# A graph network on one core: slots are released by VectorE's additions, and TensorE posts once per part of its sums

## The reference, cut to what matters

```python
q = (h @ Wq.T + bq)[dst]; k = (h @ Wk.T + bk)[src]; v = (h @ Wv.T + bv)[src]
alpha = jnp.sum(q * k, axis=-1) / 4.0          # per head, 8 heads of 16
ex = jnp.exp(alpha - segment_max(alpha, dst)[dst])
out = segment_sum(ex / segment_sum(ex, dst)[dst] * v, dst)
```

## Time and profile before

| | us |
|---|---|
| timed runs, median of 3 | 5662.24 (5661.85 to 5665.38) |
| profiled execution, span from first to last instruction | 7864.5 |

### The profile page before, as it was taken

The page is one execution under the profiler, slowest core; times in us unless marked ns, Lnnn a source line. Parts: engine busy times, 40 slices in busy tenths (PEclk is TensorE's granted clock), DMA queues, the critical chain, the costliest instruction groups (busy, mean ns, idle before and its releaser), DMA issues.

```text
span 7864.5 us, 105863 instructions
## 1 busy us (share of the span) xinstructions
PE 4591.8 (58%) x22799; PEld 3687.8 (47%) x22800; DVE 4054.1 (52%) x11127; ACT 2762.9 (35%) x6393; POOL 3848.5 (49%) x4061
## 2 busy tenths in 40 slices
PE   4555555655555556555555565555555655666666
PEld 2444444534444445344444453444444544555555
DVE  4555555645555556455555564555555653333334
ACT  1333333423333334233333342333333432333333
POOL 3555555335555553345555543455555425555553
PEclk6666666676666666766666667666666677878788
DMA  4222222122222222222222222222222211111111
GB/s 127 78 78 74 78 78 77 52 66 76 78 77 79 76 79 57 65 69 77 77 79 77 79 61 68 68 78 78 78 76 80 60 31 44 44 45 45 45 44 27
DMA packets 267185, 536.12 MB, mean 68 GB/s; under 512 B 116251, under 2 KB 148687, under 8 KB 266507
## 3 DMA queue, kind: packets, MB, share of 16 engines
q0 software_dynamic: 180992, 490.24, 23.2%
q1 hardware_dynamic: 78899, 35.89, 1.8%
q10 hardware_dynamic: 6936, 6.69, 0.3%
HBM read 512.41 MB, written 18.03 MB: 67 GB/s over the span
## 4 chain that ended last, share of the span: by engine, by line
PE 27%; another core or an unknown queue 25%; issue 20%; DVE 17%; ACT 5%; DVEq 4%; ACTq 1%; DMA 0%; SPq 0%; POOL 0%; POOLq 0%
PE bank L765 9%; PE bank L784 8%; DVE acc L1191 6%; PE bank L769 2%; PE bank L756 2%; ACT oh L549 2%; DVEq L330 2%; PE bank L805 2%; PE bank L833 1%; DVE alpha L1214 1%; DVEq L1191 1%; DVE slots L1283 1%; DVE oh L1175 1%; PE bank L937 1%
## 5 line engine op out<-in xcount | busy, mean ns | idle before, releaser
L504 POOL DMA_INDIRECT slots<-kv_table,idx x3224 | 3065.0, 951 | 3149.1 <-PE bank L784 1272.7
L784 PE MATMUL bank<-slots,oh 128*128 128x136 f32 (+1 forms) x8060 | 1598.6, 352 | 584.7 <-DVE acc L1191 502.7
L765 PE MATMUL bank<-qs,ohT 128*128 x8080 | 1676.3, 354 | 230.3 <-ACT ohT L540 132.0
L784 PEld LDWEIGHTS bank<-slots,oh 128*128 128x128 f32 x8060 | 1415.4, 253 | 716.9 <-DVE acc L1191 614.8
L765 PEld LDWEIGHTS bank<-qs,ohT 128*128 128x128 f32 x8080 | 1428.7, 256 | 450.4 <-issue 428.3
L1191 DVE TENSOR_TENSOR acc<-acc,bank 128x136 f32 (+1 forms) x4030 | 1173.6, 291 | 603.7 <-PE bank L784 166.4
L1208 DVE TENSOR_TENSOR slots<-slots,bank 128x512 f32<-128x512 f32 x808 | 552.3, 684 | 1312.1 <-remote 1294.4
L540 ACT ACTIVATE ohT<-bank,miss 128x512 f32<-128x512 f32 x1010 | 676.5, 683 | 1360.0 <-PE bank L756 1226.6
L504 POOL DMA_INDIRECT slots<-src_table,idx x806 | 760.8, 944 | 750.5 <-DMA idx<-src_e 233.6
L549 ACT ACTIVATE oh<-iota,rel_e 128x128 f32<-128x128 f32 x3168 | 962.9, 387 | 0.0
L797 PE MATMUL bank<-ident,alpha 128*128 128x128 f32 x204 | 93.7, 459 | 1459.5 <-DVE alpha L1214 1423.0
(11 more groups left out here) (255 smaller groups left out, 4032.7 us busy)
## 6 DMA issues: line engine op xcount, KB each, us to landing
slots<-kv_table,idx POOLq DMA_INDIRECT x3224
kv_table<-slots SPq DMA_DIRECT2D x20, 660.0 KB, 3.4
slots<-src_table,idx POOLq DMA_INDIRECT x806
resets<-flat_len ACTq DMA_DIRECT2D x51, 128.0 KB
idx<-src_e SPq DMA_DIRECT2D x255, 8.0 KB
terms<-flat_rel SPq DMA_DIRECT2D x255, 12.0 KB
resets<-flat_rst SPq DMA_DIRECT2D x2, 1551.0 KB
w<-in_w SPq DMA_DIRECT2D x8, 256.0 KB
```

The costliest lines, as they stand in the source:

```text
L504: pool.indirect_dma_start(slots[:, k, t, 0:width], None, table, bass.IndirectOffsetOnAxis(ap=idx[:, k, t:t + 1], axis=0))\
L765: mm = pe.matmul(o, ohT[:, j % 2, t, :], qs[:, blocks[j * G + t], 0:HID], start=True, stop=basis is None)
L784: mm = pe.matmul(bank[6 + part % 2][:, o:o + width], oh[:, k % 2, t, :], slots[:, k, t, HID:HID + width], start=True, stop=True)
```

## The change

The sixteen semaphores `slot_free` go. TensorE posts `part_ps` at the end of each of the six parts, and VectorE waits for it at the first place of each part. In the message pass VectorE's wait before the one-hots becomes a wait for three parts. GpSimd fetches the first four chunks of a pass without a wait for slots (they are a piece of code of their own), and before each later group it waits until VectorE has added the places that the slots held (`acc_done`); the numbers to wait for are kept in registers, one for each group of a chunk (`past`), and one for each ring place for the indices (`staged`). At the end it waits for all additions once.

```diff
             def gather_chunk(k, turn, l, table, width, places=CH):   # before
-                pool.wait_ge(tab_out, 16 * NI * (l + 1))
-                pool.wait_ge(idx_in[k], 16 * (turn + 1))
...
-                        pool.wait_ge(slot_free[k][j], START + used[j])
-                        pool.reg_add(uses[k][j], uses[k][j], 1)
+            def await_added(before, j, chunks):
+                pool.wait_ge(acc_done, START + (j + 1) * G + before[j])
+                pool.reg_add(past[j], past[j], CH * chunks)
+            def gather_chunk(k, l, first, table, width, places=CH, to_next=(1,) * NG):
+                groups = -(-places // G)
+                before = [pool.snap(past[j]) for j in range(groups)]
+                if first:
+                    if k == 2:
+                        pool.wait_ge(su_termsd, 48)
+                    if k == 3:
+                        pool.wait_ge(su_rstd, 16 * 2 * HEADS)
+                    pool.wait_ge(tab_out, 16 * NI * (l + 1))
+                pool.wait_ge(idx_in[k], 16 + pool.snap(staged[k]))
+                pool.reg_add(staged[k], staged[k], 16)
                 for j in range(groups):
+                    if not first:
+                        await_added(before, j, to_next[j])
                     for t in range(j * G, min((j + 1) * G, places)):
                         pool.indirect_dma_start(...)
+            def gather_pass(l, table, width):
+                for k in range(RING):
+                    gather_chunk(k, l, True, table, width)
+                with pool.Fori(1, FULL):
+                    for k in range(RING):
+                        gather_chunk(k, l, False, table, width)
...
+            for passed in past:
+                pool.wait_ge(acc_done, START + pool.snap(passed))
...
@@ add_up (TensorE)
-                    if t % G == G - 1 or (last and t == LAST_PLACES - 1):
-                        mm.then_inc(slot_free[k][j], 1)
-                    elif t == end - 1:
-                        mm.then_inc(part_ps, len(WITHIN) if last else 1)
+                    if t == end - 1:
+                        mm.then_inc(part_ps, len(PARTS) - part if last and part == parts[-1] else 1)
@@ add_place (VectorE)
-                if t == first and (end % G == 0 or (last and end == LAST_PLACES)):
-                    j = (end - 1) // G
-                    dve.wait_ge(slot_free[k][j], START + turn_of(l, i, k, j) + 1)
-                elif t == first:
-                    dve.wait_ge(part_ps, START + len(WITHIN) * g + WITHIN.index(part) + 1)
+                if t == first:
+                    dve.wait_ge(part_ps, START + len(PARTS) * g + (len(PARTS) if last and part == LAST_PARTS[-1] else part + 1))
@@ message_step (VectorE)
                 if ahead > 1:
-                    dve.wait_ge(slot_free[k][1], START + turn_of(L, i, k, 1) + 1)
+                    dve.wait_ge(part_ps, START + len(PARTS) * g + 3)
                     onehots(n + 1, k, c + 2, 0, LAST_HALVES if is_last(i, k + 2) else 2)
```

More of the change, by code:

```diff
@@ L67 @@
 PARTS = ((0, 3), (3, 6), (6, 9), (9, 12), (12, 14), (14, 16))
-WITHIN = [m for m, (_, end) in enumerate(PARTS) if end % G]
 LAST_PARTS = [m for m, (first, _) in enumerate(PARTS) if first < LAST_PLACES]
@@ L71 @@
 assert PARTS[LAST_PARTS[-1]][1] == LAST_PLACES and len(LAST_PARTS) > 1
-assert LAST_HALVES == 1 and LAST_PARTS[0] in WITHIN and LAST_NG > 1
+assert LAST_HALVES == 1 and LAST_NG > 1
 assert NB % BW == 0 and REM > 1 and FULL % ROUNDS == 0
@@ L265, in build_program @@
         kv_in = [sems(f"kv_in{k}_", NG) for k in range(RING)]
-        slot_free = [sems(f"slot_free{k}_", NG) for k in range(RING)]
         oh_far = sem("oh_far")
@@ L289, in build_program @@
                    scale_done, shift_done, shift_spread, silu_done, spread_used, sq_done, t_in,
-                   t_out, t_ps, w_done,
-                   *[s for ring in slot_free for s in ring]]
+                   t_out, t_ps, w_done]
         def is_last(i, k):
@@ L482, in _ @@
                                         bass.IndirectOffsetOnAxis(ap=vti[:, c:c + 1], axis=0)).then_inc(su_rows, 16)
[L483 to L488, removed]
-                groups = -(-places // G)
[L490 to L494, removed]
-                pool.wait_ge(tab_out, 16 * NI * (l + 1))
-                pool.wait_ge(idx_in[k], 16 * (turn + 1))
-                for j in range(groups):
-                    if isinstance(turn, int):
-                        pool.wait_ge(slot_free[k][j], START + turn)
-                    else:
-                        pool.wait_ge(slot_free[k][j], START + used[j])
-                        pool.reg_add(uses[k][j], uses[k][j], 1)
+            past = [pool.alloc_register(f"past{j}") for j in range(NG)]
+            staged = [pool.alloc_register(f"staged{k}") for k in range(RING)]
+            for r in (*past, *staged):
+                pool.reg_mov(r, 0)
+            def await_added(before, j, chunks):
+                pool.wait_ge(acc_done, START + (j + 1) * G + before[j])
+                pool.reg_add(past[j], past[j], CH * chunks)
+            def gather_chunk(k, l, first, table, width, places=CH, to_next=(1,) * NG):
+                groups = -(-places // G)
+                before = [pool.snap(past[j]) for j in range(groups)]
[7 more added lines that the diff above has]
+                pool.reg_add(staged[k], staged[k], 16)
+                for j in range(groups):
+                    if not first:
+                        await_added(before, j, to_next[j])
                     for t in range(j * G, min((j + 1) * G, places)):
@@ L506, in gather_chunk @@
                             .then_inc(kv_in[k][j], 16)
-            def gather_rest(l, table, width):
+            def gather_pass(l, table, width):
[4 more added lines that the diff above has]
+                        gather_chunk(k, l, False, table, width)
                 for k in range(REM):
-                    gather_chunk(k, turn_of(l, FULL, k), l, table, width, min(CH, PLACES - (RING * FULL + k) * CH))
+                    places = min(CH, PLACES - (RING * FULL + k) * CH)
+                    ends = [k == (REM - 1 if j < LAST_NG else REM - 2) for j in range(NG)]
+                    gather_chunk(k, l, False, table, width, places,
+                                 [CHUNKS - (RING * FULL + k - RING) if end else 1 for end in ends])
             with pool.Fori(0, L) as l:
[L513 to L520, removed]
+                gather_pass(l, kv_table, KVW)
+            gather_pass(L, src_table, HID)
+            for passed in past:
+                pool.wait_ge(acc_done, START + pool.snap(passed))
             def root(sums, out, nth):
```

## The result

| | before | after |
|---|---|---|
| timed runs, median of 4, us | 5662.49 (5661.85 to 5665.38) | 5687.14 (5684.99 to 5691.28) |
| ratio, after to before | | 1.0045 [1.0033, 1.0058] |
| span of the profiled execution, us | 7864.5 | 5683.9 (time of that execution 5685.68) |

The change costs 24.7 us, 0.45%. The direction was the forecast's, the size was not: 88 us had been forecast.

A forecast was written before the change was run, and what follows sets the result against it. The prediction took GpSimd's fetches, 1.25 us apart, as the floor of the timed passes. With (a) and (b) at 0, (c) 13 and (d) 75 summed to 88 us, 5662 + 88 = 5750 us; range 5668 to 5810.

The forecast's parts named there:

- What bounds the kernel: Whole kernel: without the late posts GpSimd's fetches, 1.25 us each, are the floor, and timed passes must be near it.
- 5802: Whole kernel: total of five passes at 948 us and 1061.5 us outside them, 2.5% above the timed median.
- (a): TensorE's posts: 6 a chunk in place of 8, taken as 0; bounds 0 to 56 us gained.
- R3: TensorE's posts: fewer posts pay, saving 31 us; 5640 us if the message-pass delay is covered too; chance 0.06.
- (b): GpSimd's own instructions: moved waits and regrouped register steps are hidden under the fetch before; 0.
- (c): Start of attention passes: slot release waits for VectorE's additions, nothing hides it; first fetch 3.2 us later, four passes, 13 us.
- R4: GpSimd's new waits: register work that is not hidden, 0.3 x 255 = 77 us; chance 0.04.
- (d): Message pass: VectorE's wait before the one-hots moves to place 8; 2.7 us per chunk, partly covered; 75 us taken, ends 3 and 132.
- The 948: Floor of one pass: 742 x 1.25 = 928 us from its first released slot, and some 20 us for the last chunk.
- the 116: Message pass: 49 x 21.2 + 25 = 1064 us in place of 948, so 116 more.
- R1: Message pass: fetches cover the delay, loop stays below 20.0 us at full clock; not slower, 5662 to 5670 us; chance 0.11.
- R2: Message pass: the loop is already the bound when timed; the full 132 us, 5794 to 5807 us; chance 0.17.

## Why the prediction was right or wrong

**What bounds the kernel: right.** The recording was stretched, the posts seen late in it, by 3.8 and 6.0 us, are not late in an undisturbed one (in before with fewer fetches the second message begins at 5007.68, 0.04 us behind the end of its products), and fetches 1.25 us apart are the floor. From the first fetch behind the ring's 64 to the last addition the undisturbed message pass takes 1019.8 - 80 = 940 us, where the floor was 948. But the 1061.5 us outside the passes were taken over from the stretched recording, where the new one of before has 707, and the attention passes take 969 to 995 from their first addition rather than 948. The two errors run against each other, so that 5802 came within 2.5% of the median partly by luck.

**(a) Fewer posts, 0: right** for the time, by the run with a post for place 7, whose interval ends at 0.9992, 5 us below before; R3 falls with it. The Trainium skill ("TensorE: Matmul & The Clock Gate", section on the cost of the per-tile semaphore tail) gave 13 us by estimate, which no run here shows. Whether TensorE itself gains anything was not tried: the fetches would hide it.

**(b) GpSimd's own instructions, 0: right**, by the run with its code alone. GpSimd is the bound there, so that tenths of a microsecond per group would have been seen; R4 falls.

**(c) The release by additions, 13 us: wrong, it is 0** by the same run. The step that failed is "At a pass's start nothing does": it took the 46.28 us of the earlier trace rows for a sign that the ring is full when the first slots are released. Undisturbed, the addition of place 3 ends at 1237.69, and the first fetch that needs it begins at 1264.78, 64 fetches of 1.25 us behind the first. The run with the release a whole chunk later shows how much room there is.

**(d) The wait for place 8: right in place and order, wrong in size: 75 us were put down, and the whole loss is 24.7.** All that was to be seen was there: one-hots behind the product of place 8, messages in a pair, the attention passes as before (in pass 2 the last fetch begins 1010.4 us behind the first in the new recording of before, at 2195.06, and 1008.3 after, at 2192.87). The delays of 2.5 and 2.7 us to the second message and the third group measure 2.6 and 2.9. What failed is the step from this delay to what the fetches leave uncovered, in three terms.

The first is the own loop of before, "some 18.5 us at the clock of that chunk". It is 17.07, at a clock of 0.90; the 18.5 was worked out from a stretched chunk in a pass at 0.81. The fetches' 20.0 stood, so the cover is 20.0 - 17.07 = 2.9 us per chunk, twice the 1.5 assumed.

The second is the price per chunk, 3.4 (20.47 - 17.07) rather than 2.7, which makes the new loop 20.47, not 21.2. At a like clock the loops are 20.00 (0.91) and 17.06 (0.90): that difference is the 2.9 of the third group's delay. The other 0.5 is the chunks in which the clock falls to 0.84. 49 times what 20.47 has above 20.0 gives 23 us, close to the 25 measured; at 0.91 throughout, by the same working, the loop would be no longer than the fetches take. That is an estimate: no run holds the clock.

The third is a count, and goes back to the step that failed in (c). The 948 has 742 fetches, 46.4 chunks, ahead of the first release, as if the ring were full then, and sets 49 chunks of the loop against them. Undisturbed the first additions of the pass begin 25.4 us behind its first fetch (4613.36 and 4588.00), with some 21 fetches issued and 785, 49 chunks, still to come. So by the forecast's own loops the delay is 49 x 1.2 = 59 us; 52 of the 116 came from that count, and 5 more from the tails. The 75 between the ends took back some of that, not all.

Where the lag ends up had not been seen either. GpSimd never waits for it: 49 times 0.5 us is 1.2 chunks, and the ring holds four. The loop falls behind fetches that keep their pace, and shows as 40 us of work behind the last one.

**Rivals.** 5687 lies in the forecast's own class, 5678 to 5790, near the end at which the fetches cover all but 3 us. R1 (covered, as the loop stays below 20.0) comes near in mechanism: 17.07 + 2.9 is 20.0, and what is above it comes with the chunks at 0.84; its time, up to 5670, is passed. R2 (uncovered, 132) is wrong for this kernel, but is what the runs with fewer fetches show, at 170. The 5640 of R3 does not follow from its terms: 5662 - 31 is 5631, with the 13 of (c) 5644. The range was to run from R1's upper edge to R2's upper end; these are 5670 and 5807, not 5668 and 5810.

**The profiled span** was forecast at 8000 to 8060; it is 5683.9. That the next recording would be stretched as well was an assumption, and it was not, so the windows of after can be read only against the new recording of before.

## What to carry to other kernels

Set the span of a profile against the timed runs before a row of it carries a term: in a stretched recording ring, waits and loops all look different, and what can be kept is the durations and the order. With a producer at a fixed pace, a delay in the consumer's loop costs only what lifts the loop above that pace, so that the consumer's own loop has to be known to a few per cent, at the clock that it runs at; leaving out some of the producer's work measures it. When a semaphore is merged with a later one, look at the long instruction that now stands at the head of an in-order queue, and move it behind something that waits for the same thing anyway.

## What was not expected of the hardware

One recording of before spans 7864.5 us, beside 5662 timed; the same program recorded again spans 5659.1, and each variant's recording is within 2 us of that execution's time. What stretched the first is open; it was not the program, which the second recording has unchanged. And chunks of one loop, with the same instructions, took 18.37 us at a granted clock of 1.00, 20.00 at 0.91 and 21.28 at 0.84, while the chunks with a later wait all had 0.92: a wait that moved 0.67 us back in each of 49 chunks cost 3 us, within the noise, rather than 33. In the changed kernel the chunks at the lower clock make up what the loop has above 20.0; in the one with the later wait their absence pays for the wait. Both come from setting profiles side by side, not from a run that holds the clock.
